# Self attention's first block of four tiles projected and placed during the last slots of cross attention

## The reference

```python
x = x + xattn(layernorm(x), ctx, ctx, mask, ...)   # 16 heads of 8, 257 keys per sequence
x = x + attn(layernorm(x), W_qkv, b_qkv, W_out, b_out)
x = x + ffn(layernorm(x), router_w, ...)           # 4 layers of 4 experts, the best 2 per token

def attn(x, W_qkv, b_qkv, W_out, b_out):           # 16 heads of 8, the 32 tokens of a sequence
    q, k, v = split(x @ W_qkv + b_qkv)
    attn = softmax(einsum('bqhe,bkhe->bqhk', q, k)) / sqrt(128)
    return einsum('bihv,bvhd->bihd', attn, v).reshape(B, N, 128) @ W_out + b_out
```

## Time and profile before

| | |
|---|---|
| median of 3 runs | 1513.58 us (1511.32 to 1515.71) |
| the profiled execution | 1515.81 us, of which the span is 1513.3 us |
| TensorE / VectorE / ScalarE / GpSimd busy | 88% / 80% / 73% / 46% |
| mean granted TensorE clock | 0.953 of full |

### The profile page before, as it was taken

The page is one execution under the profiler, slowest core; times in us unless marked ns, Lnnn a source line. Parts: engine busy times, 40 slices in busy tenths (PEclk is TensorE's granted clock), DMA queues, the critical chain, the costliest instruction groups (busy, mean ns, idle before and its releaser), DMA issues.

```text
span 1513.3 us, 46107 instructions
## 1 busy us (share of the span) xinstructions
PE 1332.4 (88%) x15863; PEld 1011.9 (67%) x15863; DVE 1218.0 (80%) x3466; ACT 1102.6 (73%) x1844; POOL 701.2 (46%) x464
## 2 busy tenths in 40 slices
PE   5898999999985499978888798999999999898988
PEld 3576777777764289945666566666676667666666
DVE  6899888898887578877878877787878788888785
ACT  3697999999975155547777676786877777777776
POOL 6276777777778233322332223433344344332333
PEclk9998999999996599999999899999999999999999
DMA  5975776676640488600000000000000000000000
GB/s 154 239 192 147 187 189 179 179 187 182 179 108 6 115 210 190 157 1 1 2 1 0 0 1 2 0 0 0 0 0 0 0 0 0 2 7 14 7 14 15
DMA packets 196201, 108.46 MB, mean 72 GB/s; under 512 B 89741, under 2 KB 194029, under 8 KB 196077
## 3 DMA queue, kind: packets, MB, share of 16 engines
q1 hardware_dynamic: 122032, 84.65, 20.5%
q10 hardware_dynamic: 74044, 22.17, 6.7%
HBM read 67.62 MB, written 39.03 MB: 70 GB/s over the span
## 4 chain that ended last, share of the span: by engine, by line
DVE 20%; PE 14%; issue 12%; ACT 5%; DVEq 1%; ACTq 0%
PE pair L1644 7%; PE pair L1626 6%; DVE hs L1557 4%; ACT gf L1499 3%; ACT gh L1504 2%; DVE xc L1531 2%; DVE rs L52 1%; DVE rs L50 1%; DVE gl L1543 1%; DVE st L1522 1%; PE pair L1656 1%; DVE rs L48 1%; DVE rs L37 1%; DVE mv L1526 1%; DVE sel L1609 1%
## 5 line engine op out<-in xcount | busy, mean ns | idle before, releaser
L1486 POOL TENSOR_TENSOR gl<-gf,gh 128x1024 f16<-128x1024 f32 x128 | 291.0, 2273 | 551.0 <-ACT gh L1504 551.0
L1499 ACT ACTIVATE gf<-pair,b1c 128x512 f32<-128x512 f32 x512 | 327.3, 680 | 153.3 <-PE pair L1626 152.7
L1644 PE MATMUL pair<-w2p,gh 128*128 (+1 forms) x4096 | 368.0, 222 | 12.3 <-DVE gl L1543 12.3
L1644 PE MATMUL pair<-w2p,gl 128*128 (+1 forms) x2048 | 359.2, 222 | 0.0
L1644 PEld LDWEIGHTS pair<-w2p,gh 128*128 128x128 f16 x4096 | 327.4, 100 | 38.3 <-issue 9.2
L1626 PE MATMUL pair<-xh,w1p 128*128 128x512 f16 x1024 | 327.8, 381 | 4.5 <-DVE w2p L1273 2.9
L335 POOL TENSOR_TENSOR pl<-p,ph 128x1024 f16<-128x1024 f32 x128 | 272.8, 2132 | 125.7 <-ACT ph L392 125.4
L1504 ACT ACTIVATE gh<-gf 128x1024 f16<-128x1024 f32 x256 | 270.6, 1057 | 24.6 <-ACT gf L1499 0.7
L1543 DVE TENSOR_TENSOR gl<-gf,gh 128x1024 f16<-128x1024 f32 x128 | 167.6, 1309 | 124.1 <-ACT gh L1504 122.0
L1644 PEld LDWEIGHTS pair<-w2p,gl 128*128 128x128 f16 x2048 | 203.9, 100 | 0.0
L1626 PE MATMUL pair<-xl,w1p 128*128 128x512 f16 x512 | 195.3, 381 | 0.0
(11 more groups left out here) (219 smaller groups left out, 2522.0 us busy)
## 6 DMA issues: line engine op xcount, KB each, us to landing
KS<-k_parts_dram SPq DMA_DIRECT2D x64, 384.0 KB, 4.5
k_parts_dram<-kh SPq DMA_DIRECT2D x64, 256.0 KB, 3.6
cx<-in_ctx_dram ACTq DMA_DIRECT2D x30, 512.0 KB, 4.5
k_parts_dram<-kl SPq DMA_DIRECT2D x64, 128.0 KB, 3.8
w1p<-in_L_ffn_w_dram SPq DMA_DIRECT2D x8, 512.0 KB, 5.7
w2p<-in_L_ffn_w_dram SPq DMA_DIRECT2D x8, 512.0 KB, 8.2
QS<-q_parts_dram ACTq DMA_DIRECT2D x128, 24.0 KB
Q<-q_parts_dram SPq DMA_DIRECT2D x32, 96.0 KB
```

Of the source, the lines that this page charges most:

```text
L1486: pool.tensor_tensor(gl[u.m2][:, 0:h, :], gf[u.m2][:, 0:h, :], gh[u.m2][:, 0:h, :], ALU.subtract).then_inc(d_loP, 1)
L1499: act.activation(gf[u.m2][:, c, :], hb[c][:, :], ACT.Gelu, scale=1.0 / WS, bias=b1c[:, u.step.expert(u.e), c]).then_inc(d_g, 1)
L1644: last = pe.matmul(yb[v.m2][:, t * D:(t + 1) * D], g[:, c, t * P:(t + 1) * P], w2p[:, le, part, c, :].rearrange("p a h -> p (a h)"), start ...
```

## The change

Slot by slot the kernel now does for block 0, with FIRST = B - 15 = 113:

- Slots 10, 14, ...: VectorE gathers the moments of one tile (tiles 0 to 30 in this way), behind the sums of the slot.
- Slot 111: VectorE runs the twelve steps of the chain over the first EARLY = 26 tiles, behind that. Slot 112: it normalises block 0 (four instructions).
- Slot 113: TensorE transposes; ScalarE copies. Slots 114 and 116: queries and keys are projected, ScalarE writes the high halves; in slots 115 and 117 VectorE writes the low halves. Slot 115: values. These stand behind the row scores of their slot on TensorE, and use `WB`.
- SyncE writes them to DRAM in slots 116 to 118, and places Q2[0], K2[0], V2[0] in slot 121 of its stream.
- GpSimd fills Q2[0] and V2[0] ahead of its slots in cross attention, in the prologue. In self attention it fills Q2[1] and V2[1] when `xm` of block 1 has been written.
- Self attention's steps leave out the work of block 0 (`fresh`). On VectorE step -2 normalises block 1; then come bv2R, WoutM, the moments of tile 31, the chain for tiles 26 to 31, and boutR (`prepare`). TensorE waits for WoutM and boutR only in step 0. SyncE starts its loads after one fill.
- Tiles and semaphores of block 0 move to the outer scope.

```diff
@@ cross attention, SyncE @@
+                    if s in (FIRST + 3, FIRST + 5):
+                        write_queries_keys(sp, 0, 0, 0, (s - FIRST - 3) // 2)
+                    if s == FIRST + 4:
+                        write_values(sp, 0, 0)
+                    if s == FIRST + 8:
+                        sp.wait_ge(a_fill, 3 * QR + 6)
+                        sp.wait_ge(c_wr[0], 16 * 2 * PARTS)
+                        place_queries_keys(sp, 0)
+                        sp.wait_ge(c_vw[0], 16)
+                        place_values(sp, 0)
@@ cross attention, GpSimd, ahead of the slots @@
                 pool.wait_ge(a_fill, 3 * QR + 4)
+                pool.memset(Q2[0][:, :, :, :, :].rearrange("p g h q b -> p (g h q b)").bitcast(F32), 0.0).then_inc(a_fill, 1)
+                pool.memset(V2[0][:, :, :, :], 0.0).then_inc(a_fill, 1)
@@ cross attention, ScalarE, behind the values of the slot @@
+                    if s == FIRST:
+                        act.wait_ge(c_xT, 1)
+                        act.activation(xmT[:, :], WB[0][:, :], ACT.Copy).then_inc(c_xTc, 1)
+                    if s in (FIRST + 1, FIRST + 3):
+                        k = (s - FIRST - 1) // 2
+                        act.wait_ge(c_pq, k + 1)
...
+                        act.activation(out, src, ACT.Identity, bias=bqk_c[:, k:k + 1]).then_inc(c_hi, 1)
+                    if s == FIRST + 2:
+                        act.wait_ge(c_pv, 1)
+                        act.activation(vn[0][:, :, :], WB[0][:, :].rearrange("p (t c) -> p t c", t=4), ACT.Copy).then_inc(c_vn, 1)
@@ cross attention, VectorE @@
                         sums(m)
+                    t = pack(s - 10)
+                    if t is not None:
+                        dve.wait_ge(c_st, t + 1)
+                        dve.bn_aggr(mv2[:, t, :], st2[:, t, :]).then_inc(c_ln, 1)
+                    if s == FIRST - 2:
+                        dve.wait_ge(c_ln, EARLY)
+                        inverse_deviation(dve, rs2[:, 0:EARLY], rw2[:, 0:EARLY], rt2[:, 0:EARLY], mv2[:, 0:EARLY, 1], c_ln, EARLY)
+                    if s == FIRST - 1:
+                        normalised(dve, 0, lambda k: slice(k, k + 1))
+                    if s in (FIRST + 2, FIRST + 4):
...
+                        dve.wait_ge(c_hi, k + 1)
+                        dve.scalar_tensor_tensor(lo, src, bqk_c[:, k:k + 1], hi, ALU.add, ALU.subtract).then_inc(c_lo, 1)
@@ cross attention, TensorE, behind row scores, keys and values @@
+                    if s == FIRST:
+                        pe.wait_ge(c_xm, 4)
+                        pe.wait_ge(kl_done, B // 2)
+                        for k in range(4):
+                            last = pe.transpose(WB[0][:, k * P:(k + 1) * P], xm[:, k, :], ident[:, :])
+                        last.then_inc(c_xT, 1)
+                    if s in (FIRST + 1, FIRST + 3):
...
+                        pe.matmul(WB[1][:, :], Wqkv[:, k * D:(k + 1) * D], xmT[:, :], start=True, stop=True).then_inc(c_pq, 1)
+                    if s == FIRST + 2:
...
+                        last.then_inc(c_pv, 1)
@@ self attention, SyncE @@
-                    sp.wait_ge(c_pool, 5)
+                    sp.wait_ge(c_pool, 1)
@@ self attention, GpSimd @@
                     pool.memset(rows[:, :], 0.0).then_inc(c_pool, 1)
-                    for i in range(2):
-
-                        pool.memset(Q2[i][:, :, :, :, :].rearrange("p g h q b -> p (g h q b)").bitcast(F32), 0.0).then_inc(c_pool, 1)
-                        pool.memset(V2[i][:, :, :, :], 0.0).then_inc(c_pool, 1)
+                    pool.wait_ge(c_xm, 8)
+                    pool.memset(Q2[1][:, :, :, :, :].rearrange("p g h q b -> p (g h q b)").bitcast(F32), 0.0).then_inc(c_pool, 1)
+                    pool.memset(V2[1][:, :, :, :], 0.0).then_inc(c_pool, 1)
@@ self attention, VectorE @@
-                    dve.wait_ge(c_st, NT)
-                    for t in range(NT):
-                        dve.bn_aggr(mv2[:, t, :], st2[:, t, :]).then_inc(c_ln, 1)
-                    dve.wait_ge(c_ln, NT)
-                    inverse_deviation(dve, rs2[:, :], rw2[:, :], rt2[:, :], mv2[:, :, 1], c_ln, NT)
-                    normalise(Tokens4(0, 0))
...
+                    def prepare():
+                        dve.tensor_scalar(bv2R[:, :], bv2_c[:, 0:1].broadcast_to((P, D)), float(D) ** -0.5, None, ALU.mult).then_inc(c_wm, 1)
+                        for j in range(GH):
+
+                            dve.tensor_scalar(WoutM[:, j, :], Wout[:, :], rowsel[:, j:j + 1], float(D) ** -0.5,
+                                              ALU.mult, ALU.mult).then_inc(c_wm, 1)
+                        dve.wait_ge(c_st, NT)
+                        dve.bn_aggr(mv2[:, NT - 1, :], st2[:, NT - 1, :]).then_inc(c_ln, 1)
+                        dve.wait_ge(c_ln, NT + RSTD_STEPS)
+                        late = slice(EARLY, NT)
+                        inverse_deviation(dve, rs2[:, late], rw2[:, late], rt2[:, late], mv2[:, late, 1], c_ln, NT + RSTD_STEPS)
+                        dve.wait_ge(c_b, 1)
+                        dve.tensor_tensor(boutR[:, :], bank[7][:, 0:D], boutR[:, :], ALU.add).then_inc(c_wm, 1)
@@ self attention, TensorE @@
-                    pe.wait_ge(c_wm, 6)
...
+                        if isinstance(st.s, int) and st.s == 0:
+                            pe.wait_ge(c_wm, 6)
@@ self attention, all engines @@
+                    step(Step(0, -2))
+                    if prepare:
+                        prepare()
+                    for s in range(-1, 1):
```

171 lines of the change are left out of this document (102 added, 69 removed).

## The result

The changed kernel takes 1490.83 us (median of 4 runs, 1489.48 to 1492.92), the kernel before beside it 1512.45 us (4 runs, 1510.16 to 1515.71): ratio 0.9857, 95% interval 0.9833 to 0.988. The forecast was 1502.8 us, its range 1494.5 to 1510.5; the gain is twice the one worked out, and the time lies 3.7 us beyond the range.

A forecast was written before the change was run, and what follows sets the result against it. VectorE was taken as the bound from 431 to 462 us, followed by a 34 us hole with no engine busy. 25.1 - 3.5 - 0.3 - 10.5 = 10.8 us less gave a median of 1502.8 us, range 1494.5 to 1510.5.

The forecast's parts named there:

- The price of holding in the tail: Tail of cross attention: inserted VectorE instructions, partly held by GpSimd, cost 10.5 us, between 5 and 14, gathered moments left out.
- The chain: Tail, slot 111: twelve steps take 8.0 us on VectorE, 5.3 of them holding by two pl of GpSimd.
- xm: Tail: the four normalising instructions of block 0 cost 1.0 us on VectorE, with no holding counted.
- The low halves and waits: Tail: two low halves, 1.35 us and not held, plus two short VectorE waits for high halves, 0.6 us.
- The prologue: Prologue: a GpSimd fill holds a VectorE chain step and delays L695, moving everything by 3.5 us, between 0 and 5.3.
- The hole: Start of self attention, before the first softmax maximum: 25.1 us less, between 22.3 and 27.6, with fills holding the chain.
- theory 1: The prediction's rule: any VectorE instruction meeting a GpSimd instruction is held to its end; hole 10.5 to 11 us with later fills.
- The steady slots: Steady slots of cross attention: VectorE's wait for ScalarE takes the gathered moments; 0.3 us counted for two in the tail.
- Rival 1: Prologue, tail, hole: no holding to speak of, the tail's chain falls into gaps; 20.6 us gained, 1493 us; chance 0.15.
- the mark of 495: End of cross attention: ending before 495 us would prove the prediction wrong in favour of rival 1; 501 was forecast.
- Rival 2: Tail: chain in lockstep with GpSimd, each step waiting for its own pl, 25.6 us; kernel slower, 1520 us; chance 0.07.
- Rival 3: Start of self attention: TensorE's low-clock ramp lasts 5 us longer or block 1 comes late; 1508 us; chance 0.16.

The follow-up runs named there:

- moments_alone: Kernel before, with only the moments of tiles 0 to 30 gathered slot by slot in cross attention; 1510.68 us, ratio 1.0007.
- The second chain: Changed kernel with the twelve chain steps run twice in slot 111, the second time over the same values; 1493.26 us (one execution).
- four_later: Changed kernel with all work of block 0 in cross attention moved four slots later, chain over 27 tiles in slot 115; 1487.17 us, ratio 0.9842.
- fills_late: Changed kernel with GpSimd's fills of Q2[1] and V2[1] waiting for the late chain's third step; 1489.58 us, ratio 0.9866.
- Spread: Changed kernel with the first chain (22 tiles) in portions of three steps in slots 94, 98, 102, 106, xm in slot 110; 1510.42 us, ratio 1.0004.
- after_again: Changed kernel, nothing edited, profiled a second time; 1492.05 us.
- the probe: Separate kernel without the layer: eight VectorE forms alone and beside GpSimd fills, tensor_tensor, copies; tensor_scalar 128x32 0.17 us alone, 1.65 to 1.74 beside fills.

## Why the prediction was wrong

**The price of holding in the tail** is the step that failed by most: 10.8 us were put down for the tail, with the gathered moments, and it cost 5.8. The prediction took VectorE as the bound by its busy time and added up the new instructions as the price, each with a holding of its own, 5.3 us for the chain alone, and let only 0.5 us of the present holding fall away. The runs show in its place that the holding in the tail is 14.9 us before and 15.2 after, while the bare work grew by some 5.5. Against moments_alone, where it is 12.6, it grew by 2.6 us; the 5.8 us are made of 7.9 for the rest of the change (10.5 predicted) and a tail 2.1 us shorter with the gathered moments (0.3 longer predicted). Holding moves from one instruction to another: in slot 115 the join of the kernel before has L527 with 1.77 us and L539 with 2.01, the changed kernel has 0.78 and 0.13 for the same two (453.90 and 455.24). On GpSimd's row the same price is 12 us of waits where there were 6.5. The second chain, with no holding, shows the bare price directly (2.6 us).

**The chain, 8.0 us predicted, 5.3 measured.** That it empties GpSimd by stopping TensorE was right, and it ends there. But the times of the two `pl` were taken from the kernel before, the second from 437.82; with the chain in the way it did not come until 442.57. One whole `pl` held it in slot 111, not two. Of the 5.3 us that GpSimd then waits, 1.2 us stood there before. In slots 115 and 119 the predicted picture did come, two steps of 2.0 to 2.1 us each, 6.6 and 6.5 us in all.

**xm, 1.0 predicted, 3.19 on VectorE**: held by one `pl`, 2.1 us, which is what the rule of the Trainium skill quoted in the prediction (GPSIMD Engine Reference, "Key points") would give. The row maximum behind it (445.46) is the one for which TensorE then waits 2.75 us, and GpSimd's wait of 4.05 us comes behind the next two `pl`. What xm costs in the tail by itself no run shows: in four_later it wasn't held, but the chain had moved as well.

**The low halves and waits, 1.95 predicted.** The halves were not held (0.75 us each), the wait for the first high half was 0.70 us. What GpSimd idles behind 448 us is 5.6 against 5.15 before, so that xm, the low halves and the detour of TensorE over transposes and projections together cost some 0.5 us more than the waits that were there. Their shares stay open.

**The prologue, 3.5 us predicted, 0 measured.** The fill came where the prediction put it (31.37), and the chain step and L797 were not held. This is the second step that failed. "A VectorE instruction that meets a GpSimd instruction is held until that one ends" is the sentence that failed, for two-input forms beside fills. The rows of the kernel before would have allowed doubt: the held instructions of the earlier trace rows beside the fills of the earlier trace rows are both `tensor_scalar`, the one-input form.

**The hole, -25.1 predicted, -25.0 measured**, on a path with a wrong victim. One `tensor_scalar` held through both fills, with eleven chain steps behind it, or the four WoutM held with twelve steps behind them, give the same sum. That the agreement is of this kind only fills_late showed: with theory 1 it could not have been 7.5.

**The steady slots, 0 predicted, 0 measured** within the microsecond by which slot 110 moves of itself: right, and moments_alone has the slots at the same 7.0 and 6.2 us. Spread shows that the reason would not carry three instructions that can be held. (The 0.3 us put down under this head were for two gathered moments in the tail; five stand there, and with them alone the tail was 2.1 us shorter.)

**The rivals.** Rival 1 has its prologue (1) and its tail (6) nearly right and its hole (27.6) wrong; at 1493 it came nearest, and cross attention ends at 491.9 us, on rival 1's side of the mark of 495. Its reason, that the chain falls into gaps, is not what the tail shows. Rival 2, lockstep: the chain was held by one whole `pl`. Rival 3, the ramp: scores 0 to 4 are 19.0 us apart (497.78 to 516.75) where they were 15.0, at the limit that the prediction named, but scores 0 start 4.6 us ahead of the first maximum now, and self attention as a whole takes 0.2 us more. It fell.

**The mixture, 3.1 us that no step named.** In the fourteen executions without the chain in slots 94 to 106 it takes 857.4, 854.3 and 854.6 us with the hole of the kernel before, and 852.4 to 853.8 with the short hole. In the first of them the granted clock is 0.89 at 1015.9 to 1025.9 us, where the changed kernel has 1.00 at the same distance. Time at half clock can be part of it and isn't shown to be: added up over the mixture it is 58.7, 58.0 and 58.6 us in the first three, 53.7 to 58.1 in the others, and 57.4 in after_again, whose mixture is 852.7 all the same. Why the short hole should go with a shorter mixture was not tried, and stays open. The terms missed are 3.5 (prologue), 5.0 (tail) and 3.1 (mixture), 11.6 us; hole and self attention were each a little worse than forecast, and so the spans are 22.0 us apart and not 10.8. The range had room for either of the first two at its end, not for both and the third.

## What to carry to other kernels

Before pricing work that is moved into a busy stretch, add up the idle time of each engine there, and the time that instructions are already held. New instructions that are held may take the holding from others: here 4.7 us were held on the new ones, and the total over the tail went from 14.9 us (12.6 with the gathered moments alone) to 15.2. Then try other places, since the total depends on the place: slot 115 in place of 111 gave 3.5 us, slot 119 nothing. Keep it in one piece and ahead of the instructions that would otherwise be held (55.0 us of tail in place of 58.0), and don't put it in portions into the gaps of a full loop (some 21 us for 3.8 us of work). Where two engines hold one another, pair the forms: here moving two fills behind seven `tensor_scalar`, of which four had been held, made the hole 3.0 us shorter for one added wait.

## What the runs showed of the hardware

What a VectorE instruction pays beside GpSimd depends on both forms. Beside a fill, `tensor_scalar` 128x32 took 1.65 to 1.74 us in place of 0.17, `tensor_tensor` and `scalar_tensor_tensor` with two SBUF inputs 0.19 as alone. Beside a GpSimd `tensor_tensor` all of these took up to 2.3 us, beside its copies 0.95 to 1.03. The forms with an input in PSUM, and the reciprocal, took their bare time beside all three. A held instruction ends just behind the GpSimd instruction (436.88 beside 436.84 in the tail of the changed kernel). The loss was up to that one's length, and for several instructions in a row more: four WoutM lost 4.7 us beside two fills.

The Trainium skill (GPSIMD Engine Reference, "Key points") names two kinds of VectorE instructions that contend: those in a two-port mode and those with two SBUF inputs. Beside `pl` the probe agrees for both. The sentence doesn't say what the GpSimd instruction does, and here that decides: beside fills, which read nothing, the kind with two SBUF inputs took 0.19 us as alone, and only the first kind was held. Which forms have the two-port mode, the Trainium skill says under VectorE: DVE Perf Modes ("The perf-mode tier table"): copies and `tensor_scalar` with both ends in SBUF, not `tensor_tensor`, and none that reads PSUM. For the forms that the table names the held and free rows beside fills divide in just this way; it doesn't name `scalar_tensor_tensor` and the reciprocal, which were free.

The mixture took 852.4 to 863.1 us with the same code, the longest in the two kernels whose cross attention was stretched. The granted clock goes with it at the two ends: the time at half clock in the mixture is 53.7 us in the first trace of the changed kernel (852.4 us) and 67.3 in spread (863.1). A difference of 3 us in a stage that no edit touches is not to be counted as gain or loss.
